# Second layer: where the GpSimd queue issues the last group's eight gathers

## The reference, cut to what matters

```
x = x + _L0_xattn_ref(_layernorm(x, axis=-1), ctx_1024, ctx_1024, mask_Bx1xS2_ik1, ...)
x = x + _L0_ffn_ref(_layernorm(x, axis=-1), ...)
x = x + _L1_xattn_ref(_layernorm(x, axis=-1), ctx_1024, ctx_1024, ...)
x = x + _L1_ffn_ref(_layernorm(x, axis=-1), ...)
```

```
scores = jax.nn.softmax(x @ gate_w + gate_b, axis=-1)
weights, indices = jax.lax.top_k(scores, K)
gathered = jnp.take_along_axis(out_bted, indices[..., None], axis=2)
routed = jnp.sum(weights[..., None] * gathered, axis=2)
```

## Time and profile before

| | |
|---|---|
| median of 3 runs | 754.68 us |
| the runs | 752.0, 754.68, 754.7 us |
| the profiled execution's own time | 749.47 us |
| its span in the profile | 747.7 us |
| mean granted TensorE clock | 0.997 of full speed |
| busy: PE, PEld, DVE, ACT, POOL | 727.4, 560.2, 462.2, 311.0, 271.7 us |
| DMA, mean over the span | 152 GB/s |

### The profile page before, as it was taken

One profiled execution on the slowest core, in us unless ns is written; L12 is line 12 of the kernel. 1 busy time (PEld: TensorE's weight loads), 2 busy tenths in 40 slices (PEclk: granted clock), 3 DMA queues, 4 the chain that ended last, 5 costly groups with the idle time before them and its releaser, 6 DMA issues.

```text
span 747.7 us, 15572 instructions
## 1 busy us (share of the span) xinstructions
PE 727.4 (97%) x5802; PEld 560.2 (75%) x5802; DVE 462.2 (62%) x1052; ACT 311.0 (42%) x556; POOL 271.7 (36%) x320
## 2 busy tenths in 40 slices
PE   8999999999999999999999999999998999999996
PEld 6776667666766575699999998989766667677774
DVE  4678663557355668534444655738677868788625
ACT  1323211422142121245555554644246755565571
POOL 5976225423410624402201515124734435205051
PEclk9999999999999999999999999999999999999998
DMA  9898944631521595722453423454887776755001
GB/s 263 224 301 265 203 117 154 187 122 41 180 71 52 188 374 171 250 59 82 118 143 88 126 76 95 121 143 133 244 223 193 183 184 175 199 140 127 28 3 50
DMA packets 73069, 113.87 MB, mean 152 GB/s; under 512 B 14930, under 2 KB 59347, under 8 KB 71075
## 3 DMA queue, kind: packets, MB, share of 16 engines
q1 hardware_dynamic: 60928, 80.17, 37.4%
q10 hardware_dynamic: 5906, 17.03, 8.4%
q0 software_dynamic: 6160, 15.67, 6.7%
HBM read 84.27 MB, written 28.41 MB: 151 GB/s over the span
## 4 chain that ended last, share of the span: by engine, by line
PE 87%; DVE 4%; POOL 2%; ACT 2%; issue 1%; DMA 1%; another core or an unknown queue 1%; ACTq 0%; SPq 0%; DVEq 0%; POOLq 0%
PE ps L1463 15%; PE ps L1092 12%; PE ps L1472 7%; PE ps L1109 7%; PE ps L2186 5%; PE ps L2215 5%; PE ps L1128 5%; PE ps L2206 4%; PE ps L1140 3%; PE ps L1062 3%; PE ps L1034 3%; PE ps L2179 2%; PE ps L2160 2%; DVE mxh L1836 2%; PE ps L1069 2%; PE ps L2115 2%
## 5 line engine op out<-in xcount | busy, mean ns | idle before, releaser
L1836 DVE TENSOR_REDUCE mxh<-ps 112x2 f32<-112x750 f32 x128 | 115.1, 932 | 34.2 <-PE ps L2186 31.3
L1463 PE MATMUL ps<-rowsT,w 128*128 128x128 f32 x1120 | 130.8, 275 | 0.0
L1463 PEld LDWEIGHTS ps<-rowsT,w 128*128 128x128 f32 x1120 | 128.0, 192 | 0.1
L2036 ACT ACTIVATE d_pT<-ps 125x448 f32<-125x448 f32 x192 | 92.0, 549 | 46.3 <-PE ps L2206 42.0
L1092 PE MATMUL ps<-x1T,sw 128*128 128x448 f32 x256 | 101.3, 540 | 0.0
L1417 ACT ACTIVATE w<-rw 128x1024 f32 x70 | 73.8, 1056 | 64.4 <-PE ps L1463 57.3
L1092 PEld LDWEIGHTS ps<-x1T,sw 128*128 128x128 f32 x256 | 47.6, 190 | 38.8 <-issue 35.9
L1356 POOL DMA_DIRECT2D yscr<-y x35 | 19.7, 563 | 153.8 <-DVE y L1390 153.8
L1472 PE MATMUL ps<-rw,h 128*128 x280 | 66.4, 380 | 0.0
L2186 PE MATMUL ps<-kst,qst 96*112 96x375 bf16 x256 | 58.4, 332 | 3.0 <-DVE mxh L1836 1.6
L902 ACT ACTIVATE silu<-ps,sb 128x448 f32<-128x448 f32 x32 | 20.3, 634 | 96.9 <-PE ps L1092 88.9
(11 more groups left out here) (259 smaller groups left out, 1193.3 us busy)
## 6 DMA issues: line engine op xcount, KB each, us to landing
kst<-kscr SPq DMA_DIRECT2D x39, 378.0 KB, 5.3
rw<-in_rw SPq DMA_DIRECT2D x24, 512.0 KB
kscr<-ka SPq DMA_DIRECT2D x16, 567.0 KB
cT<-in_ctx_t SPq DMA_DIRECT2D x17, 378.0 KB, 4.7
ctxT<-in_ctx_t SPq DMA_DIRECT2D x16, 378.0 KB
ctxn<-in_ctx SPq DMA_DIRECT2D x16, 336.0 KB
qst<-qscr ACTq DMA_DIRECT2D x12, 448.0 KB, 7.0
rows<-xg SPq DMA_DIRECT2D x35, 128.0 KB
```

Of the source, the lines that this page charges most:

```text
L1463: last = mm(bank[1 + 2 * q + k][:, block], w12[:, k, c, block], rowsT[:, q, c * P:(c + 1) * P], start=c == 0, stop=c == C - 1)
L1836: V.tensor_reduce(mxh[:, b % 2, 2 * g:2 * g + 2], ps[0:S, p:p + 2, 0:K], axis=AX_X, op=ALU.max).then_inc(s["s_max"], 1)
L2036: A(pT[:, q % 2, k, :], bank[4 + k][0:KC, 0:QUAD * S], ACT.Exp).then_inc(s["p_ready"], 1)
```

## The change

The gathers of the last group are no longer spread over the first turns. All eight indirect DMAs are issued in a row behind `split_rest`, and `parted(pool, 2)` and `parted(pool, 3)` follow them. The waits on `p_ready`, which tied each pair of gathers to ScalarE's progress through turns 0 and 1, are gone; the gathers' own waits (for the writes to `yscr`, and for the earlier users of `yg`) stay.

```diff
@@ -1750,10 +1750,9 @@
         split_rest(pool, EARLY - 1)
         i = NG - 1
         for j in range(G):
-            if j % 2:
-                parted(pool, j // 2 + 2)
-            pool.wait_ge(s["p_ready"], (2 * j + 2) * NKC)
             gather(pool, i, j)
+        parted(pool, 2)
+        parted(pool, 3)
         for j in range(0, G, 2):
             combine(i, range(j, j + 2))
             parted(pool, j // 2 + 4)
```

## The result

| | before | after |
|---|---|---|
| median, measured beside each other | 752.84 us (19 runs) | 755.62 us (19 runs) |
| lowest, highest | 751.09, 754.7 | 752.72, 758.88 |
| the profiled execution's own time | 749.47 us | 757.03 us |
| mean granted TensorE clock of the runs | 0.997 (profiled run) | 0.990 to 0.994 |

The ratio of after to before is 1.0041, 95% interval 1.0029 to 1.0053: 3.1 us slower (the two medians lie 2.8 us apart). That is inside the range and within the 0.5% that was called "no difference", but nineteen runs on either side resolve it, and it has the other sign than the forecast's -1.35 us.

A forecast was written before the change was run, and what follows sets the result against it. TensorE, busy 727.4 of 747.7 us, was taken as the bound. Holds gone from turns 0 and 1 (-2.7) plus one new hold (+1.35) gave -1.35 us: 754.68 to 753.3 us, range 749.3 to 756.6.

The forecast's parts named there:

- the forecast: Whole kernel: gain in turns 0 and 1 less one new hold, -1.35 us, 753.3 us; chance 0.45.
- Steps 1 and 2: POOL: dropping the p_ready waits saves nothing directly; parted(2) and parted(3) behind all gathers cost 0, covered by VectorE's maxima.
- Step 3: Turns 0 and 1: TensorE completions reaching waiters late beside gathers (holds) disappear, 1.09 and 1.59 us, together -2.7 us.
- Step 4: 547.6 to 557.7 us, into turn 0: the eight gathers bring one new hold, +1.35 us, bounds 0 and 5.6.
- Step 5: DMA engines: gathers' 0.9 MB beside ACT's loads; keys of sequence 3 still land 1.2 us ahead of turn 1, cost 0.
- Rival A: Run of gathers: its holds fall where TensorE has slack, so all of the gain stays, 752.0 us; chance 0.2.
- Rival B: Turns 0 and 1: late completions have another cause or move at their old price, nothing changes, 754.7 us; chance 0.2.
- Rival C: PE to DVE chain, 550.5 to 557.7: longer run holds longer, 1.87 us per hold, 755.7 or 757.6 us; chance 0.15.

The follow-up runs named there:

- before_again: The kernel before, unchanged, profiled once more on chip 0; ratio to before 1.0007.
- before_b: The kernel before, unchanged, profiled on chip 6; ratio to before 0.9991.
- after_again: The changed kernel (after), unchanged, run once more on chip 0; ratio to before 1.0025.
- late4: Against after: first four gathers stay ahead of the turns, the other four in a row behind parted(2), beside turn 1; chip 0, ratio to before 1.0003.
- late8_c: late8 again, unchanged, on chip 15; ratio to before 1.0017.
- late8_plain: Against late8: eight plain DMAs of the same bytes instead of the indirect gathers; chip 0, ratio to before 0.9988.
- late8: Against after: all eight gathers in a row moved behind parted(2), beside turn 1; chip 0, ratio to before 1.0083.
- four: Against before: first four gathers in a row ahead of the turns, the others at their old places; chip 14, ratio 0.9996.
- single: Against after: the eight gathers issued each alone, spread from ahead of turn 0 into turn 2; chip 6, ratio to before 0.9999.
- quiet: Against after: keys of sequence 3 loaded on SP's queue, store of queries moved into turn 1; chip 0, ratio to before 1.0072.

## Why the prediction was wrong, step by step

**Steps 1 and 2** (waits on `p_ready` gone, `parted` moved: 0) held: POOL's eight gathers ran as computed, and `parted(2)` waited 12.37 us for VectorE instead of being waited for.

**Step 3** (holds gone from turns 0 and 1: -2.7 us) held on the chips with 752 us, in place and in size. Turn 1 came back from 10.61 and 10.63 to 9.01 in both traces of after (-1.6, predicted -1.59). What before loses by the end of turn 0 is 36.18 - 34.81 = 1.37 us, and 1.35 in before_again (predicted 1.09). Turn 2 gave 0.3 more, which was counted at nothing. On a chip with 747 us the step is worth nothing: before_b has no such hold in turns 0 and 1, and leaving the gathers out altogether gained nothing there three times. That was not tried on chip 0, so the 2.7 us are seen in the traces' stretches and not in a median.

**Step 4** failed ("I take one hold of the mean size in turns, 2.7 / 2 = 1.35 us", between 0 and 5.6). The place was right: turn 0 has the late completions, and no time was lost before it although the run began there. The size was not. After loses 42.26 - 34.81 = 7.45 us by the end of turn 0, after_again 4.91. Two things were mis-sized. A long run holds for longer than several pieces of 1 to 2 us: beside a tight exchange a pair cost 1.4 to 1.6 us, four in a row 14.50 - 9.01 = 5.5 (late4's turn 1), eight 4.9 to 7.5 in turn 0 and 20.05 - 9.01 = 11.0 in turn 1, each with what the clock adds. And the term had nothing for the clock: TensorE, nearly idle for 5.6 us, then worked 6.9 us at 1.2 GHz for what takes about 4.6 at 2.4.

With these sizes the sum comes near. End of turn 0 +6.08 and +3.56, turn 1 -1.6, turn 2 -0.3: +4.2 and +1.7 us, each from one pair of executions. Measured were +3.1 (1.0041) and +1.9 (1.0025) over all of them.

**Step 5** (DMA: 0) held: TensorE never waits for the keys of sequence 3 at the start of turn 1, which is clean. It had left out a smaller load, the rows of maxima (`qst<-mT`): beside busy DMA engines TensorE waited for them 1.10 us in before_b, 0.97 in late8_c and 2.28 in late8_plain. In after they cost nothing.

**Rival A** and the forecast fell with step 4. **Rival B**, nothing changes, is refuted where the comparison was made, by turns 0 and 1 that both changed. The rule of the Trainium skill ("SBUF — State Buffer", "SBUF: two separate sides") beside it, that TensorE and ScalarE never wait on anyone, is about ports and doesn't cover what happens on chip 0, where all three engines stand still for 6 us (571 to 577 in late8); in turns 0 and 1 on chips 6, 14 and 15 nothing speaks against it. **Rival C** named the mechanism and the place. It had put three holds of 1.87 us as its far end, 757.6; its middle, 755.7, is what came, by luck, as the remainder of a larger cost and a real gain.

**What stays open.** What ScalarE and VectorE wait on is not shown: a completion of TensorE that is sent late, or one that arrives late, look the same here. Shown is that on chip 0 the hold moves with the run of gathers (after_again against late8), that plain DMAs in its place don't hold (late8_plain, which also issues for less than half as long, so form and time are not told apart), that it doesn't take full DMA engines, and that nothing like it stands in the traces of three other chips. What differs between the chips is open, and the holds in the turns are not the whole of it: the last write of the expert table already stands at 528.5 to 530.3 us in the seven traces of chip 0 and at 526.6 to 529.1 in the eleven of the others. Whether more distance between gathers or only 16 rows help on chip 0 wasn't tried: single, four and both kernels with 16 rows ran on chips that don't hold. After itself wasn't run on such a chip; by late8_c, which has the run in a worse place and costs 1.3 us, it should come out near before, but that is an estimate. Whether the first comparison's chip is chip 0 isn't known; its traces have the same marks. No kernel was shown to be faster than before: the best in the order of work, four and single, are at 0.9996 and 0.9999.

## What to carry to other kernels

A run of indirect DMAs beside a tight exchange between TensorE and its readers can stop the exchange for far longer than its pieces suggest, and the stall then costs the clock as well. Four in a row cost TensorE nothing beside dense matmuls (the expert tiles, late4's first four); eight did in the one trace that has them there (quiet), so that place is better but not shown to be free. Don't cost a long run from the mean of short ones. Before a stall that the profile puts down to "remote" enters a sum, look at the same kernel on a second chip, since an experiment on a chip without the stall is clean for every theory and tells nothing apart.

## What the runs showed of the hardware that I had not expected

- The same program stalls on one chip and not on another. Eight indirect DMAs of 112 rows in a row: turn 1 takes 20.05 us on chip 0 and 9.01 on chip 15, with POOL's instructions 1.24 us apart on both. The medians of before differ too, 752.1 to 752.8 against 746.8 to 747.5 us.
- Where before takes 752 us, the holds end 0.5 to 1.9 us after POOL's last gather instruction, whether the gathers' data are still moving (after) or not (late8).
- On chip 0 the same bytes as plain DMAs don't hold turn 1 (9.01 us). POOL takes 4.22 us for eight plain ones and 9.7 for eight indirect ones.
- Half the rows in an indirect DMA hold almost as long (18.68 us), with the same 0.93 us on POOL.
- A VectorE cast of 112x16 elements takes 1.61 and 2.42 us instead of 0.2 beside a POOL memset, and TensorE waits 2.12 us behind it.
- The clock can fall without such a stall: late8_c's turn 0 lost 1.55 us to it with POOL idle. In after, in a stretch of 5.6 us with 1.16 us of work, TensorE's granted clock fell to 0.50 and was still 0.50 after 6.4 us of unbroken work behind it (569.0); 24 matmuls then took 1.32 us instead of 0.77.
